# Two single-block routing batches become one, and two closing norm groups become one

## The reference, cut to what matters

```python
logits = jnp.einsum('th,eh->te', x, router_w)            # 4096 tokens, 8 experts
topk_logits, topk_idx = jax.lax.top_k(logits, 2)
probs = jax.nn.softmax(topk_logits, axis=-1)
combine = zeros(T, E).at[arange(T)[:, None], topk_idx].add(probs)
hmid = jnp.einsum('th,efh->etf', x, w1) + b1[:, None, :]  # F = 512
y    = jnp.einsum('etf,ehf->eth', gelu(hmid), w2) + b2[:, None, :]
out  = jnp.einsum('eth,te->th', y, combine)
x    = layernorm(x + out)                                 # over the 256 features
```

## Time and profile before

| | us |
|---|---|
| median of 3 runs | 1129.92 |
| their lowest and highest | 1128.23, 1133.76 |
| the profiled execution's own time | 1123.2 |
| its span | 1121.4 |
| PE busy | 1036.0 (92%) |
| DVE busy | 721.2 (64%) |
| ACT busy | 602.1 (54%) |
| POOL busy | 291.0 (26%) |

### The profile page before, as it was taken

How to read it: one execution, slowest core, us unless ns; L and a number is a source line. 1 busy time by engine, 2 the same in 40 slices (tenths; PEclk the granted TensorE clock), 3 DMA queues, 4 the chain that set the end, 5 groups by cost and what they waited for, 6 DMA issues and landing times.

```text
span 1121.4 us, 29473 instructions
## 1 busy us (share of the span) xinstructions
PE 1036.0 (92%) x10931; PEld 768.8 (69%) x10931; DVE 721.2 (64%) x1645; ACT 602.1 (54%) x1026; POOL 291.0 (26%) x399
## 2 busy tenths in 40 slices
PE   6899999999999999999999999979787899999994
PEld 3556666666667666666666666655576799999983
DVE  4656566566667877777787878785344544446766
ACT  3466776677666665666666665554523122222335
POOL 1044223223223310000213131322355322222221
PEclk9999999999999999999999999997989899999997
DMA  8016654664562000100010010102345577789784
GB/s 302 21 31 209 196 156 135 198 183 136 168 194 51 20 13 11 49 12 11 32 41 32 31 42 12 37 13 89 125 143 161 189 212 215 214 263 312 252 301 157
DMA packets 96377, 139.28 MB, mean 124 GB/s; under 512 B 11408, under 2 KB 69136, under 8 KB 95984
## 3 DMA queue, kind: packets, MB, share of 16 engines
q1 hardware_dynamic: 89616, 114.99, 33.3%
q0 software_dynamic: 6624, 22.42, 5.5%
HBM read 76.56 MB, written 60.29 MB: 122 GB/s over the span
## 4 chain that ended last, share of the span: by engine, by line
PE 75%; DVE 10%; issue 6%; ACT 3%; DVEq 2%; SPq 2%; DMA 1%; POOL 0%; ACTq 0%; POOLq 0%
PE PS L660 11%; PE PS L681 10%; PE PS L910 6%; PE PS L894 6%; PE PS L630 6%; PE PS L734 5%; PE PS L738 5%; PE PS L805 5%; PE PS L752 5%; PE PS L779 3%; PE PS L637 2%; PE PS L768 2%; DVEq L437 2%; PE PS L633 2%; PE PS L793 2%
## 5 line engine op out<-in xcount | busy, mean ns | idle before, releaser
L1296 DVE TENSOR_REDUCE part<-PS 128x6 f32<-128x768 f32 (+1 forms) x256 | 269.9, 1086 | 118.4 <-PE PS L637 85.4
L1024 ACT ACTIVATE pT<-PS 128x768 f32<-128x768 f32 (+1 forms) x256 | 220.8, 915 | 94.0 <-PE PS L660 94.0
L1835 POOL TENSOR_SCALAR_AFFINE_SELECT pT<-pT 128x512 f32<-128x512 f32 x128 | 84.5, 661 | 278.9 <-ACT pT L1024 275.3
L910 PE MATMUL PS<-w2s,qkn 128*128 x568 | 141.0, 392 | 13.6 <-ACT qkn L1141 13.2
L660 PE MATMUL PS<-big 32*128 32x256 f32 (+1 forms) x2048 | 134.5, 376 | 20.3 <-issue 14.4
L894 PEld LDWEIGHTS PS<-x1T,big 128*128 128x128 f32 x1136 | 138.2, 193 | 4.5 <-ACT x1T L1132 0.5
L660 PEld LDWEIGHTS PS<-big 32*128 32x128 f32 x2048 | 96.7, 185 | 62.7 <-issue 61.2
L894 PE MATMUL PS<-x1T,big 128*128 128x128 f32 x1136 | 138.9, 276 | 0.1
L681 PE MATMUL PS<-pT,vaug 128*32 128x256 f32 (+1 forms) x2048 | 125.4, 362 | 8.0 <-DVE sq L1365 2.0
L910 PEld LDWEIGHTS PS<-w2s,qkn 128*128 128x128 f32 x568 | 105.4, 196 | 29.2 <-issue 17.0
L1909 POOL DMA_INDIRECT p_dram<-sq,rowid x71 | 69.8, 982 | 181.5 <-DVE rowid L1615 125.7
(11 more groups left out here) (210 smaller groups left out, 1566.7 us busy)
## 6 DMA issues: line engine op xcount, KB each, us to landing
big<-w SPq DMA_DIRECT2D x71, 512.0 KB, 4.2
xs_dram<-zrow SPq DMA_DIRECT2D x24, 1496.0 KB, 10.0
vaug<-xs_dram SPq DMA_DIRECT2D x71, 136.0 KB, 2.9
xin<-xT SPq DMA_DIRECT2D x16, 256.0 KB, 3.0
w2s<-w POOLq DMA_DIRECT2D x1, 4096.0 KB, 16.2
xb<-x SPq DMA_DIRECT2D x16, 256.0 KB, 11.6
xin<-ctxT SPq DMA_DIRECT2D x16, 256.0 KB, 2.8
rows_all<-p_dram SPq DMA_DIRECT2D x8, 512.0 KB, 5.9
```

The source lines that it names most:

```text
L910: ins = pe.matmul(moe_bank(2, j)[:, 0:E], hact[:, j % 2, c * P:(c + 1) * P], w, start=(c == 0), stop=(c == FC - 1))
L1024: act.activation(pT[:, k % 2, 2 * half:2 * half + 2, 0:wide], src, ACT.Exp).then_inc((exp_a, exp_b)[half], 1)
L1296: dve.tensor_reduce(dst, src, AX.X, ALU.max, negate=True).then_inc((max_a, max_b)[half], 1)
L1835: pool.affine_select(d, d, [[0, 2], [0, 2], [1, P]], ALU.is_ge, 0.0, base=0, channel_multiplier=-1).then_inc(masked, 1)
```

## The change

The batches of block 30 and block 31 are routed as one, at block 31's quarters. There are eight batches, and so eight groups of the last norm, all of four token tiles. `CLASSES`, the number of classes of tiles in the second table, goes from 7 to 6. The number of tiles (71), of scatters (64) and of stores (71) stays.

```diff
--- before.py
+++ after.py
@@ -54,7 +54,7 @@
 FIRST_AT, SECOND_AT, RANK_AT, PLACE_AT = (28, 26), (29, 26), (31, 27), (32, 28)
 QUARTERS = 4 * (BLOCKS - 1) + PLACE_AT[1] + 1
 
-BATCHES = {B + 1: 2, B + 3: 2, B + 5: 2, B + 7: 2, B + 9: 2, B + 11: 2, B + 13: 2, B + 14: 1, B + 15: 1}
+BATCHES = {B + 1: 2, B + 3: 2, B + 5: 2, B + 7: 2, B + 9: 2, B + 11: 2, B + 13: 2, B + 15: 2}
 ROUTED = NT * max(BATCHES.values())
 
 
@@ -583,11 +583,9 @@
                     if SEND_AT.get(group) == j:
                         send_group(group)
 
-            for group in range(GROUPS - 2, GROUPS):
-                fetch_group(group)
-                if group == GROUPS - 2:
-                    for g in range(len(SEND_AT), ENDING[0]):
-                        send_group(g)
+            for group in range(len(SEND_AT), ENDING[0]):
+                send_group(group)
+            fetch_group(GROUPS - 1)
             for group in ENDING:
                 send_group(group)
             sp.wait_ge(out_done, 16 * GROUPS)
@@ -1203,11 +1201,9 @@
             seed_group(ENDING[0])
             seed_group(ENDING[1])
             normalise_group(ENDING[0])
+            normalise_group(ENDING[1])
             seed_group(ENDING[2])
-            normalise_group(ENDING[1])
             normalise_group(ENDING[2])
-            seed_group(ENDING[3])
-            normalise_group(ENDING[3])
 
         @block.vector
         def _(dve):
@@ -1773,11 +1769,9 @@
             sum_up(ENDING[0])
             measure(ENDING[1])
             refine_roots(ENDING[0])
+            refine_roots(ENDING[1])
             measure(ENDING[2])
-            refine_roots(ENDING[1])
             refine_roots(ENDING[2])
-            measure(ENDING[3])
-            refine_roots(ENDING[3])
 
         @block.gpsimd
         def _(pool):
```

## The result

The changed kernel is slower. Its four runs have a median of 1143.64 us (1139.03 to 1144.76) against 1129.78 us for four runs of the kernel before: a ratio of 1.0096, 95% interval 1.0072 to 1.0120. Between the medians lie 13.9 us, while the ratio makes 10.9 us: with few executions the two can differ by some us. The forecast was 1133.1 us, within 0.5% of no change, range 1127.5 to 1139.5: the measured time lies outside it. Span of the profiled execution 1142.0 us (1121.4 before).

A forecast was written before the change was run, and what follows sets the result against it. PE bounded the tile loop, busy 20.00 of 20.00 us, and the change touched only the loop's ends. Quarters -0.6 plus ending +3.8 gave +3.2 us on 1129.9: 1133.1 us, range 1127.5 to 1139.5.

The forecast's parts named there:

- the quarters: Last quarters of the tile loop, including the stall for a store and the second table: -0.4 - 0.2 = -0.6 us.
- the 6.7 us: Distance of the profiled execution of the kernel before under its runs' median; forecast therefore 1133.1 rather than 1126.4 us.
- Block 30's choices: At the last quarters on DVE: with them removed the finish follows the bias directly, 3.1 us gained.
- weights: Block 30's weights, removed from DVE between first root step and next finish: 0.45 us more gained.
- The clock's rival: At block 31's transposes and second layer: shorter PE idle keeps the clock up, 1.6 us more gained, some 1130.5; chance 0.20.
- The wider batch: Block 31's choices, weights and POOL instructions on twice the elements: 0.3 us for all, between 0 and 0.6.
- Eight scatters for four: POOL's row before the store DVE awaits: four more take 5.3 us; landing 3.5 us, DVE goes on at 883.1, 0.4 earlier.
- the second table: Six classes for seven: small DVE instructions behind the stall shrink by a seventh, 0.2 us gained, between 0 and 0.5.
- Behind the last tile: Closing norm's last group, four token tiles for two: fetch, measuring, root, normalising and send add 3.8 us, between 3.6 and 5.8.
- the fetch: Last group's load behind the last tile, twice the size: 1.2 us more, about 2 if group 5's send shares the engines.
- The last send: Final output transfer of the closing norm, 512 KB for 256 KB: 2.7 for 2.2 us, 0.5 more.
- The rival of the burst paid whole: At the store behind eight scatters: landing stays 5.9 us or goes to 7.4; +5.6 to +9.1, some 1137 us; chance 0.24.

The follow-up runs named there:

- burst_again: Kernel before with block 30's four scatters held back and issued with block 31's four, eight in a row; 1.0052, sessions' slower level.
- first_after: Changed kernel with block 28 and 29's eight scatters issued one a quarter, a store behind each, instead of pairs; 1.0055 against 1.0120 for the changed kernel.
- after_third: Changed kernel, nothing edited, timed again in a session where the kernel before ran near 1118 us; 1.0022.
- after: First profiled execution of the changed kernel, span 1142.0 us; its runs had a median of 1143.64 us, ratio 1.0096.
- tail_again: Kernel before with only the closing norm's last four token tiles as one group instead of two groups of two; 1.0037, sessions' slower level.
- spaced_after: Changed kernel with six small waited-for POOL fills behind every scatter of the last two batches, DMA order kept; 1.0157.
- first_before: Kernel before with block 28 and 29's eight scatters issued one a quarter, a store behind each, instead of two; 1.0010.
- rep_after: Changed kernel, nothing edited, timed again against the kernel before; 1.0103.
- split_tail: Changed kernel with the closing norm's last four token tiles as two groups of two, both fetched when the last tile is stored; 1.0082.
- after_again: Changed kernel, nothing edited, timed again in the same session as first_after and spaced_after; 1.0120.
- burst_only: Kernel before with block 30's four scatters issued together with block 31's four, eight in a row, on the sessions' faster level; 1.0010.
- paced_after: Changed kernel with block 31's eight scatters issued in pairs between stores instead of one row; 0.9981, 1117.38 us.
- paced_all_2: Changed kernel with block 31's scatters in pairs, block 28 and 29's one a quarter, two closing groups of two; second timing, 0.9925, 1111.14 us.
- before_again: Kernel before, unchanged, run again for its profile on the sessions' slower level; 1.0000, span 1125.3 us.
- rep_before: Kernel before, unchanged, run once more with its own profile; 1.0005, 1119.55 us, span 1116.0.

## Why the prediction was wrong

The sum of the prediction agrees with what was measured where nothing else came in: on level 1118 the changed kernel measured +2.5 us (-0.7 to +5.5) for the +3.2 predicted. Some of that agreement is luck, since two misses cancel, as the terms below show: the quarters gained 1.8 us more than the sum had, and the ending cost 0.9 more. The kernel was timed on level 1130, where it is +11 to +14, and of this the prediction had no step. Nor could its rows show one. The profiled execution of the kernel before took 1123.2 us where the others of its session took 1128.2 and more, it has no wait on "remote", and it holds 11,043 records of semaphore updates, as the profiles of level 1118 do (10,947 to 11,043), and not 9,499 to 9,927, as those of level 1130. So the rows showed an execution of the kind of level 1118, and the 6.7 us that the prediction only added on at the end were the one trace of what was missing.

- **The step that failed** is the row of eight scatters, in what it does to others. I priced it by one queue: who stands behind it on POOL, and who waits for that store. On level 1130 it holds up answers of an engine that has nothing to do with that queue: +5.9 us by itself, the store's own delay included (burst_again), where the step gave at most 3.5 for the slowest landing. And "the finish would follow the bias directly" was taken for a pure gain; it also took away waits that had thinned POOL's first row, and first_after shows 7.4 us for thinning it again.
- **Block 30's choices, -3.1; weights, -0.45.** Right. On level 1118 a GELU that starts 6.5 us later than its fellow in the kernel before (834.09 for 827.62) is followed by one 3.3 us later (836.47 for 833.16): -3.2. The transposes of block 31 come 2.85 us later (844.36 for 841.51): -0.46 more.
- **The clock's rival** came true as a mechanism: in after_third these transposes follow an idle time of 1.77 us for 3.19 and the second layer takes 1.99 for 3.22 us (in after, 0.87 us and 1.99). It was among the conditions named for the prediction to be wrong. The first layer behind it comes 2.02 us later than its fellow (847.56 for 845.54), so it gave 0.8 us for the 1.6 it was priced at. The length of the idle time alone doesn't decide: in the kernel before, 1.87 us of it ahead of 822.28 were followed by a second layer of 3.66 us.
- **The wider batch.** Up to the last copy ahead of the second row the 2.02 us grow to 2.56 (877.56 for 875.00 us): +0.5 for 0.3, within its range. In all -3.9 us.
- **Eight scatters for four.** The store's issue came 10.44 us behind the first scatter (10.6 predicted), DVE's wait ended at 882.00 (883.1 predicted, in an execution of its own). The landing was 2.4 us, the lower end of the range. Of the 3.9 us gained the row took 1.5 back (4.05 us behind the kernel before on ScalarE's copies past the stall, for 2.6 ahead of it), where the sum had it take 2.9 and the second table give 0.2. Quarters: -2.4 measured, -0.6 predicted.
- **Behind the last tile, +3.8.** From the last finish to the end it was +4.5 to +4.85 in every pair of profiles. The term that was mis-sized is the fetch: +1.9 for +1.2. The prediction named about 2 for the case that group 5's send shares the engines with it, and the send was indeed issued 2.2 us behind the fetch (1129.20 for 1127.03), but no run takes it away. The last send took 0.7 for 0.5. Measuring +1.45, root -0.27 and normalising +0.98 were as predicted.
- **The rival of the burst paid whole** named the right place by the wrong mechanism. Its landing of 5.7 us or more didn't come on level 1118 (2.4 to 2.5 in after_third). On level 1130 most of the landings of this store are not on record; of the two of sixteen that are, in after, both came 2.2 us behind the issue. Its time, some 1137 us, stayed 6.6 us short of the 1143.64 measured, since it had no late first row.

The pieces on level 1130: late second row +5.9 (burst_again), late first row +7.4 (first_after), ending +4.2 (tail_again), the choices' gain -3.6 (predicted; not measured on this level by itself): +13.9, for +11 to +14 measured. Each measured piece is uncertain by 2 to 3 us, so that they add up says only that no large piece is missing.

What stays open: what in the row delays TensorE's completions. That the rate matters is shown (spaced_after), the path that is shared is not; neither DMA engines nor semaphore traffic was measured apart. Nor is it known why level 1118 is free of it, with rows of eleven to thirteen. Whether the recording of the profile takes part is a rival that no run tests: the records that are missing on level 1130 and the late answers both begin with the scatters.

## What to carry to other kernels

Where one engine issues many indirect DMAs back to back, look at every engine's waits during that row, not only at what is queued behind it, and break the row with waits that stand there anyway, if the thinned row doesn't run into the next one (as in first_before): 0.3 us of issue between DMAs is a rate, and merging the two batches doubled the time of the row here, from 5.4 to 10.4 us up to the store. A gain on one engine can close the gaps that kept another engine's row thin. And time a change of this size in more than one session, and check that the profile is of the same kind as the runs: the same pair measured 1.0022 and 1.0120.

## What the runs showed of the hardware

TensorE's transposes ended at 887.38 us and the engine that waited for them went on at 898.38, while POOL issued eleven indirect DMAs 0.30 us apart. The semaphore updates of TensorE that let DVE and ScalarE go on are themselves on record at 898.32 and 898.36 us, so it is the update that came late, not the engine that was slow to see it. This came six times of six with eight scatters and three stores in front of DVE's wait on level 1130 (after, rep_after, split_tail, burst_again, first_after, after_again; 11.8 to 14.7 us between ScalarE's copies), and in none of the four profiles with a row of eleven to thirteen on level 1118 (burst_only, paced_after, after_third, paced_all_2). The same DMAs 3.0 us apart made no answer late (spaced_after).

The two levels differ in what they leave on record. Every profile taken on level 1130, but for that first one of the kernel before, holds 9,499 to 9,927 semaphore updates and 5,635 to 5,960 landings of DMAs among them; every one of level 1118 holds 10,947 to 11,043 and 6,989 to 7,050, for programs that differ by no more than 100 of 29,500 instructions. The missing ones are mostly those of DMAs, from some 550 us on, when the scatters have begun: of the 512 updates of each of the two scatter semaphores before_again holds 299 and 186, rep_before all but one.

The level itself seems to be made of the same thing. In the unchanged kernel on level 1130 ScalarE waits on "remote" beside or just behind the last scatters of each earlier batch too; before_again, whose scatters of these batches end at 570.3, 774.6 and 808.8 us:

```profile
571.59 1.94 ACT L1024 ACTIVATE pT<-PS 128x1024 f32<-128x1024 f32 x2 [2.54 <-remote]
...
774.10 1.94 ACT L1024 ACTIVATE pT<-PS 128x1024 f32<-128x1024 f32 x2 [2.61 <-remote]
...
810.25 0.38 ACT L1132 ACTIVATE x1T<-PS 128x256 f32<-128x256 f32 x1 [3.24 <-remote]
```

There are five such waits ahead of ScalarE's exponentials (2.40 to 2.61 us) and the one at 810, and none in the profiles on level 1118. At this copy the kernel before is 8.2 us later on level 1130 (810.25 us for 802.06 in rep_before). That these short waits make the level is argued from their place, not shown.
